# A scan with sums over a head's channels: gathers on column strips, one scan a step, products in pairs

## The chip, the cores and the metric

The kernel runs on one core of a Trainium2 chip. It is one long program of twelve stages, one after another, that keep the activations in SBUF from stage to stage. The metric is the device time of one execution in microseconds; the profile shows one execution instruction by instruction.

## The reference, cut to what matters

Of the twelve stages only the eighth, the linear attention with a decaying state, is touched. Per sequence (32 of them, 32 tokens each) and head (16 heads of 16 channels) it keeps a 16x16 state `S`:

```
k = sigmoid(x_norm @ key_w.T + key_b);  v, q = split(x_norm @ vq_w.T)
for each token s:                       # per sequence, per head
    S[d, e] = k[s, d] * S[d, e] + (1 - k[s, d]) * v[s, e]
    h[s, e] = sum over d of q[s, d] * S[d, e]
x = x + h @ out_w.T + out_b
```

Written with the difference to `v`, as the kernel does it, a step over one channel `e` is: spread `v[e]` (as a difference of neighbouring tokens) to the 16 partitions of its head, run a first-order scan along the tokens with the decay `k`, multiply with `q`, and sum over the 16 partitions of the head; `v` times the sum of `q` is added at the end.

## The kernel before, in words

Tokens lie along the free dimension, 512 to a half, and channels on the 128 partitions, so 8 heads are in a chunk. The 256 channels (two chunks) and 1024 tokens (two halves) make four quarters `i` (in the code `HALVES`), and each has 16 steps `e`, one for each channel of a head; `k` counts the 64 steps. A step goes through four engines:

- TensorE spreads (`spread_out`, L2344 and L2345): a 128x128 matrix of zeros and ones times the rounded differences and their rest, for two groups of 8 sequences of 33 columns each (`BIT` is 264). Each group goes into a PSUM bank of its own; three pairs of banks (`SLOTS`) rotate, so a spread waits for the scan three steps earlier.
- VectorE scans (L2459): `tensor_tensor_scan` over 264 columns, one instruction for each bank, from PSUM into one of four `state` buffers (`RING`). Column 0 of each sequence has a decay of zero, which starts the sequence afresh.
- GpSimd multiplies the state with the query (L2317), 512 columns into one of four `product` buffers.
- TensorE gathers (`gather_in`, L2356): an fp32 product of 128x128 weights `gather[:, e, :]`, with ones that send the 16 partitions of a head to output row `e` of that head, accumulated over the 16 steps of the quarter in a bank of `SUM`. It is issued three steps (`LAG`) behind the spread.

Between the steps lies the work of a quarter: `query_sums` (L2362) sums the query over a head on TensorE after step `QSUM`, `own_values` (L2431) multiplies that with `v` on VectorE, `results` (L2437) adds both out of PSUM into `hT` at step `EVICT` of the next quarter. In the third quarter, at the steps in `OUT`, TensorE multiplies the first four token tiles with the output weights (`project`, L2366) and VectorE adds them to `x` (L2441); the other four follow behind the loop. TensorE, VectorE and GpSimd each run their queue in the order written and wait on counting semaphores (`spread_done`, `state_ready`, `product_ready`, `gathered`, `own_ready`, `hT_ready`, `y_done`, `x_done`).

Ahead of the loop come the layer norm, the loads and twelve projections. SyncE loads the weights of the two next stages once the stage's own have come (`cw.sp`, `xw.sp`).

Of the kernel before, what the change touches and what calls it, by code (L numbers as in the profile page):

```python
# [6 lines left out]
ALU = mybir.AluOpType  # L7
# [8 lines left out]
P = 128  # L16
BATCH, SEQ, D = 32, 32, 256
# [4 lines left out]
HALF = 512  # L22
# [72 lines left out]
class Norm:  # L95


    HALVES = [range(0, TILES // 2), range(TILES // 2, TILES)]
# [199 lines left out]
class QuantWeights:  # L298


    PIECES, RING, FIRST, STEPS = 12, 3, 10, 8

# [1926 lines left out]
def stage_scan(core, cw, xw):  # L2229
    nc, d = core.nc, core.dram  # L2230
    HD = 16
    HALVES = CD * 2
    OWN = HALF // SEQ
    STEP = SEQ + 1
    BITS = 2
    BIT = OWN // BITS * STEP
    SLOTS = 3
    RING = 4
    LAG = 3
    EVICT, QSUM, OUT = 4, 6, (8, 10, 12, 14)  # L2240
    with ExitStack() as ctx:
        st = Stage(core, ctx, "scan")
        ln = Norm(st, shared=True)
# [1 line left out]
        wo = st.sb("wo", [P, CD, D])  # L2245
        bk = st.sb("bk", [P, CD])
        bo = st.sb("bo", [P, D])
        gather = st.sb("gather", [P, HD, P])
        same_head = st.sb("same_head", [P, P])
        decay = st.sb("decay", [P, HALVES, OWN, STEP])  # L2250
        vT = st.sb("vT", [P, HALVES, OWN, STEP])
        dv = st.sb("dv", [P, HALVES, OWN, STEP])
        spread_r = st.sb("spread_r", [P, HD, P], F32R)
        dv_hi, dv_lo = st.sb("dv_hi", [P, HALVES, OWN * STEP], F32R), st.sb("dv_lo", [P, HALVES, OWN * STEP], F32R)
        qT = st.sb("qT", [P, HALVES, HALF])
        own_v = st.sb("own_v", [P, 2, HALF])
        state = st.sb("state", [P, RING, OWN, STEP])
        product = st.sb("product", [P, RING, HALF])
        spread = product[:, :, :].rearrange("p r (e m) -> p (r e) m", m=P)
# [13 lines left out]
        hT_ready = st.sem("hT_ready")  # L2273
        y_done, x_done = st.sem("y_done"), st.sem("x_done")
        bank = [b[:, :] for b in core.bank]
        SPREAD, SUM = [bank[0:2], bank[2:4], bank[4:6]], bank[6:8]
        PROJ = [(kind, n, c) for n in range(2) for c in range(CD) for kind in ("v", "k", "q")]
        block = ctx.enter_context(nc.Block())

# [2 lines left out]

        def by_seq(a):
            return a.rearrange("p (b s) -> p b s", s=SEQ)

        @block.sync
        def _(sp):
# [12 lines left out]
        @block.gpsimd  # L2300
        def _(pool):
            for a in (decay, vT, dv):
                nc.gpsimd.memset(a[:, :, :, 0:1], 0.0).then_inc(first_zero, 1)
            ln.pool(pool)
            pool.wait_ge(loaded, 64)
            ln.all_ready(pool)
            for t in range(TILES):
                nc.gpsimd.tensor_tensor(core.x[:, t, :], core.x[:, t, :], bo[:, :], ALU.add).then_inc(bo_added, 1)
            pool.wait_ge(proj_taken, len(PROJ))
            pool.wait_ge(spread_ready, 1)  # L2310
            for i in range(HALVES):
                for e in range(HD):
                    k = i * HD + e
                    pool.wait_ge(state_ready, (k + 1) * BITS)
                    if k >= RING:
                        pool.wait_ge(gathered, k - RING + 1)
                    nc.gpsimd.tensor_tensor(by_seq(product[:, k % RING, :]), state[:, k % RING, :, 1:STEP], by_seq(qT[:, i, :]),  # L2317
                                            ALU.mult).then_inc(product_ready, 1)

        @block.tensor  # L2320
        def _(pe):
# [14 lines left out]
            def spread_out(k):  # L2336
                i, e = divmod(k, HD)
                if e == 0:
                    pe.wait_ge(lo_ready, i + 1)
                if k >= SLOTS:  # L2340
                    pe.wait_ge(state_ready, (k - SLOTS + 1) * BITS)
                for g in range(BITS):
                    now, to = slice(g * BIT, (g + 1) * BIT), SPREAD[k % SLOTS][g][:, 0:BIT]
                    nc.tensor.matmul(to, spread_r[:, e, :], dv_hi[:, i, now], start=True, stop=False)  # L2344
                    nc.tensor.matmul(to, spread_r[:, e, :], dv_lo[:, i, now], start=False, stop=True).then_inc(spread_done, 1)  # L2345

            def gather_in(k):
                i, e = divmod(k, HD)
                if e == 0 and i >= 1:
                    pe.wait_ge(own_ready, i)  # L2350
                if e == 0 and i >= 2:
                    pe.wait_ge(hT_ready, i - 1)
                if k == 3 * HD:
                    pe.wait_ge(x_done, len(OUT))
                pe.wait_ge(product_ready, k + 1)
                nc.tensor.matmul(SUM[i % 2], gather[:, e, :], product[:, k % RING, :], start=(e == 0),  # L2356
                                 stop=(e == HD - 1)).then_inc(gathered, 1)

            def query_sums(i):
                if i >= 1:  # L2360
# [11 lines left out]
            for k in range(HALVES * HD + LAG):  # L2372
                i, e = divmod(k, HD)
                if i < HALVES:
                    spread_out(k)
                if k >= LAG:
                    gather_in(k - LAG)
                if i < HALVES and e == QSUM:
                    query_sums(i)
                if i == 2 and e in OUT:  # L2380
                    t = OUT.index(e)
                    if t == 0:
                        pe.wait_ge(own_ready, 3)
                    else:
                        pe.wait_ge(x_done, t)
                    project(t, SUM[1])
# [32 lines left out]
        def _(dve):  # L2419
# [12 lines left out]

            def results(i):
                n, c = divmod(i, CD)
                dve.wait_ge(gathered, (i + 1) * HD)
# [9 lines left out]
            for k in range(HALVES * HD):  # L2445
                i, e = divmod(k, HD)
                if i >= 1 and e == EVICT:
                    results(i - 1)
                if e == QSUM + 1:
                    own_values(i)  # L2450
                if i == 2 and e - 1 in OUT:
                    add(OUT.index(e - 1), SUM[1])
# [1247 lines left out]
```

## Time and profile before

| | us |
|---|---|
| median of 3 runs | 1755.07 |
| lowest and highest run | 1753.1, 1763.58 |
| profiled execution, first to last instruction (span) | 1752.7 |
| busy over the span: TensorE, VectorE, ScalarE, GpSimd | 1579.5, 1061.8, 846.3, 773.6 |
| the 128 scans (L2459), first start to last end | 1193.21 to 1285.06 |

The profiled execution is not one of the three runs, and of its own time the span is what is given. Times in the rows count from the start of that span. PE is TensorE's matmul part, DVE is VectorE, ACT ScalarE, POOL GpSimd and SP SyncE; an fp32 matmul leaves two records. Matmuls are pipelined, so a record is longer than the distance to the next, and it is that distance, the pitch, which shows what a stream of them costs. PEclk is the granted TensorE clock as a share of 2.4 GHz.

### The profile page before, as it was taken

The page shows a single profiled execution, that of the slowest core. Times are in us where ns is not written, and L with a number is a line of the kernel's source. Part 1 is how long each engine was busy: PE and PEld are TensorE (multiplying, and loading weights), DVE is VectorE, ACT ScalarE, POOL GpSimd, SP SyncE. Part 2 cuts the span into 40 slices and gives each one's busy share as a digit, 9 for nine tenths or more (in the row PEclk, how much of TensorE's full clock was granted, in tenths as well). Part 3 has the DMA queues.
Part 4 walks back from the last instruction along what each step waited for, and adds up shares of the span by engine and source line. Part 5 has one row for each costly group of instructions (what it writes and reads, how often), then busy time and mean ns, then how long its engine had stood idle before and what let it go on. Part 6 is the DMA issues. An engine that isn't in the chain of part 4 may idle for free. (4 is left out here: it accounts for less than half of the span.)

```text
span 1752.7 us, 37478 instructions
## 1 busy us (share of the span) xinstructions
PE 1579.5 (90%) x13621; PEld 1342.1 (77%) x13621; DVE 1061.8 (61%) x2990; ACT 846.3 (48%) x2433; POOL 773.6 (44%) x926
## 2 busy tenths in 40 slices
PE   7999999888888999987999999989978978759998
PEld 6889898757557999966888888955648834539997
DVE  5887887456866888844877666738960232263332
ACT  5766666445336888842756666641003213114332
POOL 7655665243339999833211111226734311212332
PEclk9999999999998999999999999999989977879999
DMA  8555545120014343303533333335037263871221
GB/s 267 181 163 169 162 153 164 58 85 2 1 37 158 128 140 134 119 19 111 176 109 103 112 121 104 104 113 176 1 88 240 25 194 127 269 237 30 39 39 28
DMA packets 127223, 205.32 MB, mean 117 GB/s; under 512 B 21034, under 2 KB 92363, under 8 KB 126531
## 3 DMA queue, kind: packets, MB, share of 16 engines
q1 hardware_dynamic: 119016, 189.62, 33.3%
q0 software_dynamic: 6720, 8.79, 3.2%
q10 hardware_dynamic: 1306, 4.51, 0.8%
q8 instruction: 112, 1.84, 0.4%
q14 instruction: 69, 0.56, 0.1%
HBM read 162.54 MB, written 41.14 MB: 116 GB/s over the span
## 5 line engine op out<-in xcount | busy, mean ns | idle before, releaser
L883 DVE TENSOR_SCALAR xattn_oT<-banks,xattn_last 128x256 f32<-128x256 f32 x256 | 111.8, 478 | 90.5 <-PE banks L703 90.4
L789 ACT ACTIVATE xattn_probs<-banks,xattn_negmax 128x257 f32<-128x257 f32 x256 | 124.0, 484 | 61.4 <-DVE xattn_negmax L864 61.3
L794 ACT ACTIVATE xattn_probs<-xattn_probs,xattn_rsum 128x257 f32<-128x257 f32 x256 | 131.9, 515 | 1.4 <-DVE xattn_rsum L868 1.4
L1114 POOL TENSOR_SCALAR xattn_probs<-xattn_probs,xattn_rsum 128x257 f32<-128x257 f32 x128 | 119.9, 937 | 21.3 <-DVE xattn_rsum L1354 21.2
L864 DVE TENSOR_REDUCE xattn_negmax<-banks 128x1 f32<-128x257 f32 x256 | 106.6, 416 | 35.1 <-PE banks L676 33.5
L621 POOL COPY ctx_stat<-xattn_mv 128x2 f32<-128x2 f32 x32 | 6.0, 189 | 238.1 <-DVE xattn_mv L897 238.1
L873 DVE TENSOR_TENSOR xattn_probsT_lo<-banks,xattn_probsT_hi 128x256 fp32r<-128x256 f32 x256 | 105.1, 410 | 9.8 <-ACT xattn_probsT_hi L800 8.8
L800 ACT CAST xattn_probsT_hi<-banks 128x256 fp32r<-128x256 f32 x256 | 95.6, 374 | 31.7 <-PE banks L683 27.7
L683 PE MATMUL banks<-ident,xattn_probs 128*128 128x128 f32 x512 | 103.7, 285 | 3.2 <-ACT xattn_probs L794 2.7
L672 PE MATMUL banks<-xattn_ctxT,xattn_qk_hi 128*128 128x258 f32 x256 | 93.7, 366 | 0.5 <-DVE xattn_qk L860 0.5
L577 POOL TENSOR_SCALAR xattn_ctxT<-xattn_rawT 128x514 fp32r<-128x514 f32 x32 | 49.9, 1560 | 98.1 <-issue 92.9
L698 PE MATMUL banks<-xattn_probsT_hi,xattn_ctxN 128*128 128x256 f32 x256 | 84.9, 332 | 4.9 <-DVE xattn_oT L883 3.3
L2317 POOL TENSOR_TENSOR scan_product<-scan_state,scan_qT 128x512 f32<-128x512 f32 x64 | 75.7, 1183 | 27.8 <-DVE scan_state L2459 27.3
L3051 PE MATMUL banks<-moe_xinT,moe_w_now 128*128 128x128 f32 x736 | 86.8, 277 | 0.0
L210 ACT COPY xnT<-banks 128x512 f32<-128x512 f32 x40 | 21.3, 589 | 135.0 <-PE banks L190 135.0
L3051 PEld LDWEIGHTS banks<-moe_xinT,moe_w_now 128*128 128x128 f32 x736 | 85.1, 194 | 0.1
L654 PE MATMUL banks<-xattn_qT,xattn_wk 64*128 64x128 f32 x1024 | 73.3, 283 | 12.8 <-DVE xattn_qT L849 10.0
L3009 POOL DMA_INDIRECT out_dram<-moe_y_slots,moe_row_u x23 | 36.5, 1585 | 108.7 <-DVE moe_y_slots L3176 105.7
L3061 PE MATMUL banks<-moe_w,moe_hT 128*128 x368 | 83.1, 379 | 0.0
L2459 DVE TENSOR_TENSOR_SCAN scan_state<-banks,scan_decay 128x264 f32<-128x264 f32 x128 | 81.3, 689 | 1.3
L654 PEld LDWEIGHTS banks<-xattn_qT,xattn_wk 64*128 64x128 f32 x1024 | 62.2, 187 | 22.0 <-issue 12.6
L719 PE MATMUL banks<-xattn_oT,xattn_wv 128*64 128x128 f32 x1024 | 69.4, 278 | 10.2 <-issue 7.6
(517 smaller groups left out, 5228.7 us busy)
## 6 DMA issues: line engine op xcount, KB each, us to landing
xattn_ctxT<-ctx_partsT SPq DMA_DIRECT2D x64, 516.0 KB, 4.0
xattn_ctxN<-ctx_partsN SPq DMA_DIRECT2D x64, 384.0 KB, 4.1
ctx_partsT<-xattn_ctxT SPq DMA_DIRECT2D x32, 516.0 KB
moe_w<-in_L_ffn_W SPq DMA_DIRECT2D x16, 1024.0 KB, 13.8
ctx_partsN<-xattn_ctxN SPq DMA_DIRECT2D x32, 384.0 KB
moecap_w_early<-in_L_ffn_w SPq DMA_DIRECT2D x10, 1024.0 KB, 9.3
xattn_rawN<-in_ctx SPq DMA_DIRECT2D x32, 192.0 KB, 2.8
xattn_raw<-in_ctx SPq DMA_DIRECT2D x32, 192.0 KB, 4.4
```

The costliest lines, as they stand in the source:

```text
L654: mm = nc.tensor.matmul(bank[:, k * P:(k + 1) * P], wk_s[r, h // 2, g % 2 * P:(g % 2 + 1) * P], qT[r, h // 2, :], start=True, stop=True, t ...
L672: nc.tensor.matmul(out, unit(qk1[0]), part(0, 0), start=True, stop=False)
L683: mm = nc.tensor.transpose(TB[n % 2][:, c * P:(c + 1) * P], probs[:, n % RING, c * P:(c + 1) * P], core.ident[:, :])
L698: nc.tensor.matmul(OB[:, 0:2 * P], first_hi(c), hi[:, c], start=(c == 0), stop=False)
L789: nc.scalar.activation(probs[:, n % RING, :], SB[n % 2][:, 0:KV], ACT.Exp, bias=negmax[:, n % RING:n % RING + 1], accum_out=psum[:, n % RI ...
L794: nc.scalar.mul(probs[:, n % RING, :], probs[:, n % RING, :], rsum[:, n % RING:n % RING + 1]).then_inc(norm_ready, 1)
L800: nc.scalar.copy(probsT[0][:, n // 2 % PAIRS, :, n % 2, :], TB[n % 2][:, 0:2 * P].rearrange("p (c n) -> p c n", c=2)).then_inc(probsT_hi_r ...
L864: nc.vector.tensor_reduce(negmax[:, n % RING:n % RING + 1], SB[n % 2][:, 0:KV], AX.X, ALU.max, negate=True).then_inc(negmax_ready, 1)
L873: nc.vector.tensor_tensor(lo, TB[n % 2][:, 0:2 * P].rearrange("p (c n) -> p c n", c=2), hi, ALU.subtract).then_inc(probsT_ready, 1)
L883: nc.vector.tensor_scalar(oT[k][:, heads, b, :], by_head(OB[:, k * 2 * P:(k + 1) * 2 * P]), last[:, k, j * PER_TILE + b:j * PER_TILE + b + ...
L1114: nc.gpsimd.tensor_scalar(probs[:, n % RING, :], probs[:, n % RING, :], rsum[:, n % RING:n % RING + 1], None, ALU.mult).then_inc(norm_read ...
L3051: mm = nc.tensor.matmul(H[n % 2][k][:, f * P:(f + 1) * P], w1_now[:, c, at:at + P], xinT[:, n % 2, c, :], start=(c == 0), stop=(c == CD - 1))
```

## The change

- **Gathers.** One gather now takes four steps (`QUAD`): four products of 128x32 weights, each with its own step's `product`, into the 32 PSUM partitions of its own column strip (`tile_position`). Steps `e`, `e+1`, `e+2`, `e+3` go to strips 0 to 3, four quads accumulate over the quarter, and one signal stands for a quad. The output channels of a chunk come out in another order; the host permutes the value weights, the output weights, and the zero-one matrices to fit, and the `gather` table shrinks to a quarter.
- **Scan.** The two halves of a spread are written at the end of one bank and the start of the next, so that 528 columns are contiguous, and one scan reads them. One signal stands for a step in `spread_done` and `state_ready`.
- **Products.** GpSimd multiplies the states of two steps (`PAIR`) in one instruction of 1024 columns, the query repeated. Six states and eight products rotate.
- **Order.** `LAG` goes from 3 to 5 (plus the four of a quad), `results` from step 4 to 7, the query sums from 6 to 9, own values from 7 to 11, and the output products of the first four tiles from steps 8, 10, 12, 14 of the third quarter to 13, 15, 17, 19, over its end.

```diff
-    RING = 4
-    LAG = 3
-    EVICT, QSUM, OUT = 4, 6, (8, 10, 12, 14)
+    RING, PRODUCTS = 6, 8
+    PAIR, QUAD = 2, 4
+    LAG = 5
+    EVICT, QSUM, OWN_AT = 7, 9, 11
+    OUT = [2 * HD + o for o in (13, 15, 17, 19)]
...
-        gather = st.sb("gather", [P, HD, P])
+        gather = st.sb("gather", [P, HD, SEQ])
...
-        SPREAD, SUM = [bank[0:2], bank[2:4], bank[4:6]], bank[6:8]
+        SPREAD = [core.banks[:, k * BITS:(k + 1) * BITS, :].rearrange("p g n -> p (g n)")[:, HALF - BIT:HALF + BIT] for k in range(SLOTS)]
+        SUM = bank[6:8]
...
-            for i in range(HALVES):
-                for e in range(HD):
-                    k = i * HD + e
-                    pool.wait_ge(state_ready, (k + 1) * BITS)
-                    if k >= RING:
-                        pool.wait_ge(gathered, k - RING + 1)
-                    nc.gpsimd.tensor_tensor(by_seq(product[:, k % RING, :]), state[:, k % RING, :, 1:STEP], by_seq(qT[:, i, :]),
-                                            ALU.mult).then_inc(product_ready, 1)
+            for k in range(0, HALVES * HD, PAIR):
+                pool.wait_ge(state_ready, k + PAIR)
+                if k >= PRODUCTS:
+                    pool.wait_ge(gathered, (k - PRODUCTS) // QUAD + 1)
+                now, to = slice(k % RING, k % RING + PAIR), slice(k % PRODUCTS, k % PRODUCTS + PAIR)
+                query = by_seq(qT[:, k // HD, :]).unsqueeze(1).broadcast_to([P, PAIR, OWN, SEQ])
+                nc.gpsimd.tensor_tensor(product[:, to, :].rearrange("p r (b s) -> p r b s", s=SEQ), state[:, now, :, 1:STEP], query,
+                                        ALU.mult).then_inc(product_ready, 1)
...
-                    pe.wait_ge(state_ready, (k - SLOTS + 1) * BITS)
+                    pe.wait_ge(state_ready, k - SLOTS + 1)
...
-                pe.wait_ge(product_ready, k + 1)
-                nc.tensor.matmul(SUM[i % 2], gather[:, e, :], product[:, k % RING, :], start=(e == 0),
-                                 stop=(e == HD - 1)).then_inc(gathered, 1)
+                pe.wait_ge(product_ready, (k + QUAD) // PAIR)
+                for z in range(QUAD):
+                    mm = nc.tensor.matmul(SUM[i % 2][z * SEQ:(z + 1) * SEQ, :], gather[:, e + z, :], product[:, (k + z) % PRODUCTS, :],
+                                          start=(e == 0), stop=(e == HD - QUAD), tile_position=(0, z * SEQ))
+                mm.then_inc(gathered, 1)
...
-                if k >= LAG:
-                    gather_in(k - LAG)
+                if k >= LAG and (k - LAG) % QUAD == QUAD - 1:
+                    gather_in(k - LAG - QUAD + 1)
...
-                if i == 2 and e in OUT:
-                    t = OUT.index(e)
+                if k in OUT:
+                    t = OUT.index(k)
...
                 if k >= RING:
-                    dve.wait_ge(product_ready, k - RING + 1)
-                for g in range(BITS):
-                    dve.wait_ge(spread_done, k * BITS + g + 1)
-                    of = slice(g * OWN // BITS, (g + 1) * OWN // BITS)
-                    flat = lambda a: a.rearrange("p b s -> p (b s)")
-                    nc.vector.tensor_tensor_scan(flat(state[:, k % RING, of, :]), SPREAD[k % SLOTS][g][:, 0:BIT], flat(decay[:, i, of, :]), 0.0,
-                                                 ALU.add, ALU.mult).then_inc(state_ready, 1)
+                    dve.wait_ge(product_ready, (k - RING) // PAIR + 1)
+                dve.wait_ge(spread_done, k + 1)
+                nc.vector.tensor_tensor_scan(flat(state[:, k % RING, :, :]), SPREAD[k % SLOTS], flat(decay[:, i, :, :]), 0.0,
+                                             ALU.add, ALU.mult).then_inc(state_ready, 1)
```

## Rows read from the trace of the kernel before

**Rows 1.** Windows, middle of loop: stretch, busy of each engine, PEclk, DMA, GB/s

```profile
1220.00:1243.00 23.00, 23.00 (x101) 14.46 (x99) 22.08 (x36) 0.00 (x0) 19.51 (x17) 1.00 0.00 1
```

**Rows 2.** Groups by line, 1193 to 1287 us

```profile
L2459 DVE TENSOR_TENSOR_SCAN scan_state<-banks,scan_decay 128x264 f32<-128x264 f32 x128 | 81.3, 689 | 1.3
L2317 POOL TENSOR_TENSOR scan_product<-scan_state,scan_qT 128x512 f32<-128x512 f32 x64 | 75.7, 1183 | 27.8 <-DVE scan_state L2459 27.3
L2356 PE MATMUL banks<-scan_product,scan_gather 128*128 128x512 f32 x128 | 65.1, 593 | 0.6 <-POOL scan_product L2317 0.6
...
L2366 PE MATMUL banks<-scan_wo,scan_hT 128*128 128x256 f32 x16 | 4.1, 379 | 0.0
L2362 PE MATMUL banks<-scan_qT,scan_same_head 128*128 128x512 f32 x8 | 4.1, 592 | 0.0
...
L2431 DVE TENSOR_TENSOR scan_own_v<-banks,scan_vT 128x512 f32<-128x512 f32 x4 | 2.8, 691 | 1.6 <-PE banks L2362 1.6
...
L2441 DVE TENSOR_TENSOR x<-x,banks 128x256 f32<-128x256 f32 x4 | 1.7, 422 | 2.3 <-PE banks L2366 2.3
```

**Rows 3.** Timeline of PE, one step: start us, us, engine, line, idle before

```profile
1197.37 1.02 PE L2356 MATMUL banks<-scan_product,scan_gather 128*128 128x512 f32 x2
...
1198.35 0.28 PE L2345 MATMUL banks<-scan_dv_lo,scan_spread_r 128*128 128x264 f32 x1
...
1198.58 0.28 PE L2345 MATMUL banks<-scan_dv_lo,scan_spread_r 128*128 128x264 f32 x1
1198.71 1.02 PE L2356 MATMUL banks<-scan_product,scan_gather 128*128 128x512 f32 x2
```

**Rows 4.** Timeline, first spread product and first scans

```profile
1192.07 0.39 PE L2344 MATMUL banks<-scan_dv_hi,scan_spread_r 128*128 128x264 f32 x1 [0.68 <-ACT scan_qT L2410]
...
1193.21 8.47 DVE L2459 TENSOR_TENSOR_SCAN scan_state<-banks,scan_decay 128x264 f32<-128x264 f32 x14
```

**Rows 5.** Timeline, end of the loop

```profile
1282.41 2.65 DVE L2459 TENSOR_TENSOR_SCAN scan_state<-banks,scan_decay 128x264 f32<-128x264 f32 x4
...
1285.14 1.18 POOL L2317 TENSOR_TENSOR scan_product<-scan_state,scan_qT 128x512 f32<-128x512 f32 x1 [0.17 <-DVE scan_state L2459]
...
1287.53 0.69 DVE L2437 TENSOR_TENSOR scan_hT<-banks,scan_own_v 128x512 f32<-128x512 f32 x1 [2.47 <-PE banks L2356]
```

**Rows 6.** Timeline of PE, products on column strips in a later stage

```profile
1445.18 0.27 PE L3404 MATMUL banks<-ident,xattn_o_norm 128*128 128x128 f32 x1
1445.29 0.27 PE L3405 MATMUL banks<-ident,xattn_o_norm 128*64 128x128 f32 x1
1445.49 0.86 PE L3393 MATMUL banks<-xattn_N,xattn_probsT 128*32 128x194 f32 x16
...
1446.75 0.66 PE L3368 MATMUL banks<-xattn_T,xattn_qk 128*32 128x257 f32 x8
1447.21 0.64 PE L3369 MATMUL banks<-xattn_T,xattn_qk 66*32 66x257 f32 x8
1447.78 0.44 PE L3377 MATMUL banks<-ident,xattn_probs 128*128 128x128 f32 x2
```

**Rows 7.** Groups by line and shape, GpSimd, whole span

```profile
L1487 POOL TENSOR_TENSOR attn_probs<-attn_probs,attn_rsum 128x512 f32<-128x512 f32 x8 | 8.4, 1050 | 16.6 <-DVE attn_rsum L1683 16.6
...
L1784 POOL TENSOR_TENSOR attn_x_plus<-x,xn 128x2048 f32<-128x2048 f32 x1 | 4.5, 4525 | 0.6 <-DVE xn L155 0.6
```

**Rows 8.** Windows and timeline of PE in other stages

```profile
820.00:825.00 5.00, 3.06 (x20) 1.39 (x18) 3.36 (x18) 2.42 (x5) 2.69 (x4) 1.00 0.74 254
...
1305.00:1310.00 5.00, 0.42 (x8) 0.36 (x8) 4.19 (x21) 0.21 (x1) 0.00 (x0) 0.50 0.32 82
...
1465.00:1470.00 5.00, 5.00 (x27) 2.12 (x26) 0.00 (x0) 0.97 (x3) 0.33 (x2) 0.50 0.30 119
...
825.86 3.81 PE L636 MATMUL banks<-xnT,xattn_wq 128*128 128x128 f32 x32 [2.34 <-ACT xnT L210]
...
1463.60 0.47 PE L3404 MATMUL banks<-ident,xattn_o_norm 128*128 128x128 f32 x1 [1.45 <-ACT xattn_o_norm L3482]
```

More of the change, by code:

```diff
@@ L2257, in stage_scan @@
         state = st.sb("state", [P, RING, OWN, STEP])
-        product = st.sb("product", [P, RING, HALF])
-        spread = product[:, :, :].rearrange("p r (e m) -> p (r e) m", m=P)
+        product = st.sb("product", [P, PRODUCTS, HALF])
+        spread = product[:, 0:HD * P // HALF, :].rearrange("p r (e m) -> p (r e) m", m=P)
         hT = st.sb("hT", [P, CD, TOKENS])
@@ L2284, in by_seq, with flat @@
             return a.rearrange("p (b s) -> p b s", s=SEQ)
+        def flat(a):
+            return a.rearrange("p b s -> p (b s)")
         @block.sync
@@ L2340, in spread_out @@
                 if k >= SLOTS:
-                    pe.wait_ge(state_ready, (k - SLOTS + 1) * BITS)
+                    pe.wait_ge(state_ready, k - SLOTS + 1)
                 for g in range(BITS):
-                    now, to = slice(g * BIT, (g + 1) * BIT), SPREAD[k % SLOTS][g][:, 0:BIT]
+                    now = slice(g * BIT, (g + 1) * BIT)
+                    to = SPREAD[k % SLOTS][:, now]
                     nc.tensor.matmul(to, spread_r[:, e, :], dv_hi[:, i, now], start=True, stop=False)
-                    nc.tensor.matmul(to, spread_r[:, e, :], dv_lo[:, i, now], start=False, stop=True).then_inc(spread_done, 1)
+                    mm = nc.tensor.matmul(to, spread_r[:, e, :], dv_lo[:, i, now], start=False, stop=True)
+                mm.then_inc(spread_done, 1)
             def gather_in(k):
@@ L2434, in results @@
                 n, c = divmod(i, CD)
-                dve.wait_ge(gathered, (i + 1) * HD)
+                dve.wait_ge(gathered, (i + 1) * HD // QUAD)
                 dve.wait_ge(own_ready, i + 1)
@@ L2448, in _ @@
                     results(i - 1)
-                if e == QSUM + 1:
+                if e == OWN_AT:
                     own_values(i)
-                if i == 2 and e - 1 in OUT:
-                    add(OUT.index(e - 1), SUM[1])
+                if k - 1 in OUT:
+                    add(OUT.index(k - 1), SUM[1])
                 if k >= RING:
-                    dve.wait_ge(product_ready, k - RING + 1)
-                for g in range(BITS):
-                    dve.wait_ge(spread_done, k * BITS + g + 1)
-                    of = slice(g * OWN // BITS, (g + 1) * OWN // BITS)
-                    flat = lambda a: a.rearrange("p b s -> p (b s)")
-                    nc.vector.tensor_tensor_scan(flat(state[:, k % RING, of, :]), SPREAD[k % SLOTS][g][:, 0:BIT], flat(decay[:, i, of, :]), 0.0,
-                                                 ALU.add, ALU.mult).then_inc(state_ready, 1)
+                    dve.wait_ge(product_ready, (k - RING) // PAIR + 1)
+                dve.wait_ge(spread_done, k + 1)
+                nc.vector.tensor_tensor_scan(flat(state[:, k % RING, :, :]), SPREAD[k % SLOTS], flat(decay[:, i, :, :]), 0.0,
+                                             ALU.add, ALU.mult).then_inc(state_ready, 1)
             results(HALVES - 1)
@@ L3671 @@
     same_head = p[:, None] // HD == p[None, :] // HD
-    spread = same_head[:, None, :] & (p[:, None, None] % HD == np.arange(HD)[None, :, None])
-    data["spread"] = np.ascontiguousarray(spread, dtype=np.float32)
-    data["same_head"] = np.ascontiguousarray(same_head, dtype=np.float32)
-    data["gather"] = np.ascontiguousarray(spread.transpose(2, 1, 0), dtype=np.float32)
+    strip, place = p // SEQ, p % SEQ
+    at = place % (P // HD) * HD + place // (P // HD) * 4 + strip
+    chunks = np.concatenate([at, P + at])
+    vq = data["L2_attn_vq_w_T"]
+    data["L2_attn_vq_w_T"] = np.ascontiguousarray(np.concatenate([vq[:, 0:D][:, chunks], vq[:, D:]], axis=1))
+    data["L2_attn_out_w_T"] = np.ascontiguousarray(data["L2_attn_out_w_T"][chunks])
+    spread = same_head[:, None, :] & (p[:, None, None] % HD == np.arange(HD)[None, :, None])
+    data["spread"] = np.ascontiguousarray(spread[at], dtype=np.float32)
+    data["same_head"] = np.ascontiguousarray(same_head[:, at], dtype=np.float32)
+    own = np.stack([(at[e % 4 * SEQ:(e % 4 + 1) * SEQ] % HD == e)[None, :] & same_head[:, at[e % 4 * SEQ:(e % 4 + 1) * SEQ]]
+                    for e in range(HD)], axis=1)
+    data["gather"] = np.ascontiguousarray(own, dtype=np.float32)
     data["number"] = np.arange(512, dtype=np.float32)
```

## The prediction

> **What bounds the kernel now.** I read the busy shares by stretch first. In the middle of the scan loop the matmul engine is busy 23.00 of 23 us at full granted clock, VectorE 22.08, GpSimd 19.51, and the DMA engines are silent [rows 1]. All three engines are nearly full, so busy time alone doesn't name the bound. The groups by line do: GpSimd's product waits 27.3 us in total for VectorE's scan, while the scan has only 1.3 us of recorded idle time ahead of it [rows 2]. What the scan itself waits for shows in TensorE's timeline. There one step takes 1.34 us, from one gather (1197.37) to the next (1198.71), with no hole: four spread products that start 0.12 us apart (0.23 us for two, 1198.35 to 1198.58) are 0.48 us, and the fp32 gather runs as two records, 0.59 us long and together 1.02, so 0.43 us apart: 0.86 us [rows 2, 3]. So TensorE needs 64 x 1.34 = 85.8 us, plus four query sums of 0.86 us and four output products of about the same (4.1 us busy for each kind, overlaps with their neighbours counted in [rows 2]): 85.8 + 3.4 + 3.4 = 92.6 us. The loop lasts 91.9 us from the first scan at 1193.21 [rows 4] to the end of the last at 1282.41 + 2.65 = 1285.06 [rows 5]. TensorE fits.
>
> VectorE could go faster. Where spread sums lie ready, 14 scans follow each other in 8.47 us: (8.47 - 0.68)/13 = 0.60 us each, 1.20 us a step [rows 4]. Its other work in the loop is three evictions and four own-value products of 512 columns, 0.691 us, and four adds of 0.422 us, each followed 0.08 us before its recorded end as the scans are (0.68 - 0.60): 7 x 0.61 + 4 x 0.34 = 5.6 us [rows 2]. That is 76.8 + 5.6 = 82.4 us, 10.2 us below TensorE. GpSimd needs 64 x 1.18 = 75.5 us [rows 2].
>
> **The gathers on column strips.** A gather of one step fills all 128 output columns of the array's weights, though a step yields 8 useful rows. The change takes four steps as four products of 32 weight columns, each on its own strip. The records stay as many (128), so all depends on whether strips overlap. The nearest rows are the score products of a later stage: 128x32 weights, 257 columns, fp32. Eight records on four strips start at 1446.75 and the next eight at 1447.21, so 0.46 us for eight, and the sixteen are gone by 1447.78, 1.03 us [rows 6]. One after another at the gather's rate (0.43 us for 512 columns, 0.215 for 257) sixteen would take 3.44 us. Overlap is 3.3 to 3.7 of 4. Eight records of 512 columns then take 0.46 x 512/257 = 0.92 us. Going over from whole-array products to strips costs little there: a transpose at 1445.29 (0.11 us by the pitch of its neighbours) is followed by the first strip at 1445.49 [rows 6], 0.1 us late; I allow the same on the way back. A quad of steps thus costs 1.1 us on TensorE, where four gathers cost 3.44. TensorE's total falls to 64 x 0.48 + 16 x 1.1 + 6.8 = 55 us, far off the path.
>
> **One scan of 528 columns.** No row has one. VectorE's 256- and 512-column tensor operations with a PSUM operand last 0.422 and 0.691 us [rows 2], so 0.153 us of an instruction doesn't grow with its width. Two scans joined then last 2 x 0.68 - 0.153 = 1.21 us and follow each other every 1.13. Ends: 1.20 (nothing saved; the input also crosses from one PSUM bank into the next, which no row shows) and 1.05 (the 0.08 us of overlap saved once more). I take 1.13, since the two widths are the nearest rows. That a gain from joining can only be small is what the Trainium skill says too (DVE: opcode table, instruction layouts, handler registers and perf-mode slots, Datapath and trigger behaviour): the built-in scan runs at half throughput. By that rule, at the 0.96 GHz of its page Trainium Kernel Development and Optimization, NeuronCore Architecture, I estimate 264 columns at 0.55 us; the trace's pitch of 0.60 agrees and leaves 0.05 of it to save, for a joined pitch of 1.15 and a sum 1.3 us longer than the one below.
>
> VectorE's loop becomes 64 x 1.13 + 5.6 = 77.9 us against 91.9: **14.0 us less**. Its new waits cost nothing by this sum. One signal for both halves of a step delays only the first scan, and that one starts at 1193.21, over 1 us behind the first spread product at 1192.07 [rows 4], when a step's 0.48 us of them are long written. With three slots a spread may begin two scans (2.3 us) before it is read, and it takes 0.48 us, a quad 1.1 or a query sum 0.86 us between: the cover holds, and if a strip quad took over 1.7 us it would be gone. The eviction moves from step 4 to 7, its quad being issued at step 4 and done before step 6; the output products move past the half's end, one to every second step, and each finds its add done one step earlier. With those products spaced so, behind the waiting TensorE instruction stands one step's spread, not needed for over another step.
>
> **Products of two steps.** GpSimd's rows of 512 and 2048 columns, 1.183 and 4.525 us, give 2.18 ns a column and 0.07 us fixed [rows 2, 7]. A pair of 1024 columns then takes 2.30 us, 32 of them 73.5 us, under VectorE's 77.9. Ends: 2.10 (a 512-column product with a repeated operand takes 1.050 [rows 7]) and 2.37 (nothing saved). The pair's query is a repeated operand; that row speaks against a penalty. With six states, VectorE reuses a state four steps after its pair is complete, 4.5 us against 2.3: no wait. Eight products hold two quads, and a pair's place is freed by a quad issued about three steps earlier.
>
> What the pair costs is at the **end**. Now the last product begins 0.08 us behind the last scan (1285.14) and lasts 1.18; the last eviction starts at 1287.53, 2.47 us after the scans end [rows 5]. With pairs the last product is 2.30 us long, 1.1 more, and the last quad 0.1 to 0.2 us longer than one gather: **1.3 us more**. The output products behind it, and all later stages, keep their lengths; the loads of the next stages are done by the middle of the loop [rows 1], so nothing that was hidden comes out. The smaller gather table and the reordered weights touch loads and the host alone: nothing, as the loop starts behind projections on TensorE.
>
> **Sum.** 14.0 - 1.3 = 12.7 us off the profiled span of 1752.7 gives 1740.0. The median of the runs is 2.4 us above that span, which I take for what lies around it: 1742.4 us, 0.7% less.
>
> **Rivals.**
> 1. *VectorE or GpSimd takes the gain.* If the joined scan saves nothing, the loop is 64 x 1.20 + 5.6 = 82.4 us and the time 1747. If GpSimd is slow at pairs, its chain (2.3 us for the first two scans, 32 pairs, 1.3 for the last quad) passes VectorE's 77.9 + 3.8 from 2.44 us a pair; each further 0.1 us costs 3.2 us, and at 2.85 the time is that of before. For it: both engines are already at 85 to 96% busy [rows 1]. Against: GpSimd now waits for VectorE, and its two widths show a fixed part to save.
> 2. *The clock falls, and it ends slower.* TensorE would be occupied 55 of 78 us instead of all of it. Its granted clock stands at 1.00 (2.4 GHz) in a stretch with 3.06 of 5 us busy, but at 0.50 (1.2 GHz) in one with 0.42, and at 0.50 even in one with 5.00, after TensorE had waited 1.45 us [rows 8]. At half clock a step takes 0.96 + 2.1/4 = 1.49 us, all of TensorE's work 64 x 1.49 + 13.6 = 109 us; against the 95.5 us of now (1192.07 to the last eviction [rows 4, 5]) that is 13.5 us more: 1768. A step is then 109/64 = 1.70 us against 1.22 at full clock and 1.42 of now less the longer end, so it decides from two fifths of the loop at half clock on. For it: that stretch of rows 8. Against: TensorE's holes would be under 0.7 us, once a step, and behind a hole of 2.34 us at 825.86 the clock was still full [rows 8]. The Trainium skill's page TensorE: Matmul & The Clock Gate, Part 1, has throttled as the default state, which activity releases; rows 8 show both levels, so by that rule this rival stands.
> 3. *The strips run one after another* (the change then doesn't do what it says): a quad 3.6 us, a step 0.48 + 0.9 = 1.38, TensorE's work 64 x 1.38 + 6.8 = 95.1 us, 2.5 more than now, and behind the scans 1.3 us of product and 2.5 us of last quad on top: 1761. Rows 6 speak against it.
>
> **How the numbers follow.** The forecast's own band, with scan and pair between their ends, is 1738 to 1746: chance 0.73. Rival 1 (1746 to 1754): 0.15. Rival 2: 0.09, mostly in part (1750 to 1768). Rival 3: 0.03. The range 1738 to 1753 leaves out the upper parts of rivals 1 and 2, all of 3, and a little below. One per cent, about what a measurement of this kernel tells from no change, is 17.5 us: below 1737.5 needs the 1.05 scan together with 2.10 pairs or luck of the median (0.05); above 1772.6 nothing but the clock and more (0.03); within: 0.92.
>
> **What would show it.** After: 64 scans of about 1.21 us at a pitch of 1.13, GpSimd pairs of 2.30, gather records in bunches of eight within 1.1 us, TensorE waiting for the scan in most steps, clock 1.00, last eviction 3.8 us after the last scan. Wrong would be: scans with holes behind a GpSimd product, pairs above 2.44, gather records 0.43 us apart, or a granted clock of 0.50 in the loop.

## The result and the profile after

| | before | changed |
|---|---|---|
| median, us | 1761.74 (9 runs) | 1745.19 (9 runs) |
| lowest and highest, us | 1747.81, 1767.54 | 1742.32, 1759.40 |
| time of the profiled execution, us | not given (span 1752.7) | 1754.86 (span 1752.9) |

The ratio over all runs is 0.994 with a 95% interval of 0.9913 to 0.9967: 10.6 us of 1761.74 less, between 5.8 and 15.3. (The two medians alone are 16.6 us apart, the two means 11.1.) Against the forecast 0.7% it is 0.6%, and the median lies 2.8 us above the predicted 1742.4. The kernel before has a median of 1755.07 over its first three runs and of 1761.74 over all nine, so the ratio says more than the difference from one number.

The spans of the two profiled executions are equal all the same. In the one of after, the seven untouched stages ahead took 10.7 us more: the eighth begins at 1174.0 us instead of 1163.3, and over all profiled executions of this study it begins between 1162.6 and 1179.5. The total of one execution can't show a change of this size. From the first scan to the last instruction of the program the executions differ: 559.5 us before, 548.9 with the change and 548.5 for the same kernel again (e11), 10.6 and 11.0 less. But the stages behind vary too, between 455.1 and 460.0 us over the executions of the table. What shows the change best is the **stage by itself**, from the start of its first scan, and it repeats to 0.01 us (e11 against the changed kernel in the table). The first scan begins 29.9 to 30.0 us behind the stage's first VectorE instruction in all of them, so nothing of the change hides ahead of it. All times below are us from the first scan; "next stage" is the first VectorE instruction of the stage behind (its layer norm's statistics), and "end" is the stretch from the end of the last scan to the last eviction.

| kernel | last scan ends | last eviction | next stage | end | one execution |
|---|---|---|---|---|---|
| before | 91.85 | 94.32 | 99.57 | 2.47 | (span 1752.7) |
| changed | 79.08 | 83.38 | 91.37 | 4.30 | 1754.86 |
| e11_change_again | 79.08 | 83.38 | 91.36 | 4.30 | 1746.86 |
| e5_joined_alone | 91.99 | 94.46 | 99.71 | 2.47 | 1755.55 |
| e4_strips_alone | 83.24 | 85.67 | 92.50 | 2.44 | 1754.10 |
| e6_no_pairs | 80.77 | 84.08 | 91.17 | 3.31 | 1747.60 |
| e7_whole_gathers | 97.67 | 103.70 | 108.94 | 6.04 | 1767.42 |
| e1_filled_hole | 80.76 | 84.19 | 89.44 | 3.43 | 1748.42 |
| e2_single_end | 80.84 | 85.11 | 91.82 | 4.27 | 1745.93 |
| e3_both | 79.06 | 82.48 | 87.73 | 3.42 | 1742.46 |
| e8_busy_steps | 79.61 | 83.03 | 88.28 | 3.42 | 1755.30 |
| e9, e10 (e8 again) | 79.61 | 83.03 | 88.28 | 3.42 | 1746.08, 1745.54 |
| e12_single_busy | 79.58 | 82.02 | 87.26 | 2.44 | 1742.32 |

The loop is 12.77 us shorter, the end 1.83 longer, and from the last eviction to the next stage it takes 7.99 us instead of 5.25, 2.74 more: 12.77 - 1.83 - 2.74 = 8.20 us less for the stage. The groups by line of after, 1190 to 1290 us (against [rows 2]):

```profile
L2466 DVE TENSOR_TENSOR_SCAN scan_state<-banks,scan_decay 128x528 f32<-128x528 f32 x64 | 74.7, 1234 | 0.0
L2323 POOL TENSOR_TENSOR scan_product<-scan_state,scan_qT 128x1024 f32<-128x1024 f32 x32 | 70.0, 2186 | 21.6 <-DVE scan_state L2466 19.4
L2351 PE MATMUL banks<-scan_dv_hi,scan_spread_r 128*128 128x264 f32 x128 | 40.6, 340 | 13.0 <-DVE scan_state L2466 12.3 <-ACT scan_qT L2420 0.7
...
L2365 PE MATMUL banks<-scan_product,scan_gather 128*32 128x512 f32 x128 | 17.9, 633 | 3.9 <-POOL scan_product L2323 3.9
```

The scan has no idle time at all, and TensorE's spread (L2351) now waits 12.3 us for the scan. In the kernel before, the spread waited 0.8 us for it:

```profile
L2344 PE MATMUL banks<-scan_dv_hi,scan_spread_r 128*128 128x264 f32 x125 | 56.4, 471 | 0.8 <-DVE scan_state L2459 0.8
```

VectorE is the bound now. VectorE's own timeline says so directly, and gives the pitch:

```profile
1203.99 12.73 DVE L2466 TENSOR_TENSOR_SCAN scan_state<-banks,scan_decay 128x528 f32<-128x528 f32 x11
1216.64 0.67 DVE L2441 TENSOR_TENSOR scan_own_v<-banks,scan_vT 128x512 f32<-128x512 f32 x1
1217.22 13.87 DVE L2466 TENSOR_TENSOR_SCAN scan_state<-banks,scan_decay 128x528 f32<-128x528 f32 x12
...
1277.23 5.84 DVE L2466 TENSOR_TENSOR_SCAN scan_state<-banks,scan_decay 128x528 f32<-128x528 f32 x5
1287.37 0.69 DVE L2447 TENSOR_TENSOR scan_hT<-banks,scan_own_v 128x512 f32<-128x512 f32 x1 [4.30 <-PE banks L2365]
```

Eleven scans follow each other in 12.73 us: (12.73 - 1.234)/10 = 1.150 us. The next row starts 0.58 us behind 1216.64, without a hole, and no hole comes until the last eviction, which waited 4.30 us. TensorE's timeline around one gather of four steps (against [rows 3]):

```profile
1221.35 0.28 PE L2352 MATMUL banks<-scan_dv_lo,scan_spread_r 128*128 128x264 f32 x1
1221.56 1.07 PE L2365 MATMUL banks<-scan_product,scan_gather 128*32 128x512 f32 x8
1222.56 0.39 PE L2351 MATMUL banks<-scan_dv_hi,scan_spread_r 128*128 128x264 f32 x1
1222.79 0.28 PE L2352 MATMUL banks<-scan_dv_lo,scan_spread_r 128*128 128x264 f32 x1
```

The eight records of a quad take 1.07 us. From the last spread product ahead (1221.35) to the second behind (1222.79) it is 1.44 us, of which those two products are 0.24 by their pitch: a quad occupies TensorE for 1.20 us with the passages to strips and back, 0.30 a step instead of 0.86. Then the end of the stage (against [rows 5]), with the granted clock by stretch below it (columns as in [rows 1]):

```profile
1278.56 6.75 POOL L2323 TENSOR_TENSOR scan_product<-scan_state,scan_qT 128x1024 f32<-128x1024 f32 x3 [0.69 <-DVE scan_state L2466]
...
1280.79 1.07 PE L2365 MATMUL banks<-scan_product,scan_gather 128*32 128x512 f32 x8 [0.35 <-POOL scan_product L2323]
...
1285.36 1.94 PE L2365 MATMUL banks<-scan_product,scan_gather 128*32 128x512 f32 x8 [3.51 <-POOL scan_product L2323]
...
1288.11 6.47 PE L2376 MATMUL banks<-scan_wo,scan_hT 128*128 128x256 f32 x16 [0.81 <-DVE scan_hT L2447]
...
1295.36 1.41 DVE L142 BATCH_NORM_STATS2 moecap_ln_stats<-x 128x6 f32<-128x256 f32 x4 [0.32 <-PEq L2243]
```

```profile
1220.00:1230.00 10.00, 7.96 (x52) 4.85 (x50) 10.00 (x10) 0.00 (x0) 9.49 (x5) 1.00 0.01 2
...
1280.00:1284.00 4.00, 1.51 (x12) 0.39 (x10) 3.07 (x3) 0.00 (x0) 3.76 (x3) 0.93 0.00 0
1284.00:1288.00 4.00, 1.94 (x8) 0.20 (x8) 0.63 (x1) 0.00 (x0) 1.31 (x1) 0.50 0.00 0
1288.00:1296.00 8.00, 6.62 (x18) 5.04 (x18) 2.38 (x7) 0.00 (x0) 0.00 (x0) 0.64 0.00 0
```

The last scan ends at 1283.07, the last pair at 1285.31. Before the last quad TensorE has stood idle for 3.51 us, the clock is at 0.50 (1.2 GHz), and the same eight records take 1.94 us. It is still there when the output products begin: 6.47 us for sixteen. The kernel before had 3.72 for the same sixteen, at full clock:

```profile
1288.28 3.72 PE L2366 MATMUL banks<-scan_wo,scan_hT 128*128 128x256 f32 x16 [0.78 <-DVE scan_hT L2437]
```

```profile
1287.00:1293.00 6.00, 4.22 (x18) 2.96 (x16) 2.60 (x6) 0.00 (x0) 0.00 (x0) 1.00 0.00 0
```

### The profile page after: what moved, and what is told of

It reads as the page before. It is cut to its first block and busy times, and to the rows that moved or that the text cites. A ratio compares the mean times of both kernels' runs of the same rounds, so it can differ in the third digit from the quotient of the medians.

```text
span 1752.9 us, 37348 instructions
## 1 busy us (share of the span) xinstructions
PE 1559.6 (89%) x13621; PEld 1332.4 (76%) x13621; DVE 1054.2 (60%) x2926; ACT 846.2 (48%) x2433; POOL 767.9 (44%) x894
## 5 line engine op out<-in xcount | busy, mean ns | idle before, releaser
L654 PE MATMUL banks<-xattn_qT,xattn_wk 64*128 64x128 f32 x1024 | 73.3, 283 | 12.8 <-DVE xattn_qT L849 10.0
L2323 POOL TENSOR_TENSOR scan_product<-scan_state,scan_qT 128x1024 f32<-128x1024 f32 x32 | 70.0, 2186 | 21.6 <-DVE scan_state L2466 19.4
L636 PE MATMUL banks<-xnT,xattn_wq 128*128 128x128 f32 x512 | 71.2, 288 | 6.4 <-ACT xnT L210 4.2
```

What stands on the lines that cost most here:

```text
L654: mm = nc.tensor.matmul(bank[:, k * P:(k + 1) * P], wk_s[r, h // 2, g % 2 * P:(g % 2 + 1) * P], qT[r, h // 2, :], start=True, stop=True, t ...
```

## The experiments

My theory after this look: the loop is VectorE's, at 1.15 us a scan; the strips give the room, the joined scan takes it, and the pairs only add to the end; most of the missing 4.5 us is the hole of 3.5 us at the end, behind which the clock is at half. Rivals: the clock has nothing to do with the hole; the pairs are needed for the loop; the last pair is what makes the end long; one part alone would have done. `keep_busy(n, bank)` is a helper that the kernel has already: n bf16 products of 128x256 on TensorE whose result nobody reads.

**The end: hole and last pair.** Three kernels: e1 gives TensorE 24 idle products between the last quad but one and the last quad, e2 splits the last pair in two single products, and e3 does both.

```diff
 # e1, TensorE's loop, ahead of gather_in
+    if k == HALVES * HD + 1:
+        pe.wait_ge(state_ready, HALVES * HD - 2)
+        core.keep_busy(24, 2)
 # e2, GpSimd's loop
-    for k in range(0, HALVES * HD, PAIR):
+    for k in [*range(0, HALVES * HD - PAIR, PAIR), HALVES * HD - 2, HALVES * HD - 1]:
+        n = PAIR if k < HALVES * HD - PAIR else 1
```

> The changed kernel with 24 idle-work products of 128x256 bf16 on TensorE between the last quad but one and the last quad, in the 3.5 us hole. My theory: the clock fell to 0.50 at the end because TensorE had nothing to do for 3.5 us, and the half clock made the last quad 0.9 us and the output products 2.7 us longer. Then the clock stays at 1.00, the last quad takes 1.07 us instead of 1.94, the output products 3.7 instead of 6.5, and from the first scan to the next stage's first VectorE instruction it is 87.7 us instead of 91.4. Rival: the end is slow for another reason (strips at the end, the order of the banks): 91.4 as it was, or longer by the added work.

> The changed kernel with the last pair of products split into two single ones. My theory: the pair costs 1.0 us at the end (2.19 against 1.18 us), so from the first scan to the last eviction 82.4 us instead of 83.4; the hole on TensorE shrinks from 3.5 to 2.5 us, and if that is short enough for the clock the next stage begins 87 us behind the first scan instead of 91.4, else 90.4. Rival: the last quad waits for something else than the last product: 83.4 again.

> Both edits: the hole filled and the last pair split. My theory: 81.5 us from the first scan to the last eviction and 86.7 to the next stage (99.6 before the change, 91.4 with it), some 13 us less than the kernel before, a ratio of 0.9925. Rival (the end is slow for another reason): 90 to 91 us to the next stage and a ratio of 0.994 as the change.

The timeline of TensorE in e1, at its end:

```profile
1277.28 2.79 PE L50 MATMUL banks<-ident 128*128 128x256 bf16 x24
1280.85 1.07 PE L2365 MATMUL banks<-scan_product,scan_gather 128*32 128x512 f32 x8 [0.78 <-POOL scan_product L2323]
1282.73 3.72 PE L2376 MATMUL banks<-scan_wo,scan_hT 128*128 128x256 f32 x16 [0.81 <-DVE scan_hT L2450]
```

With the hole filled down to 0.78 us the quad takes 1.07 again and the output products 3.72. The end shrinks from 4.30 to 3.43, and the way to the next stage from 7.99 to 5.25, what it was before the change: 0.87 + 2.74 = 3.6 us. So the hole was the cause: of the executions on strips, in none of the six in which it is filled (e1, e3, e8, e9, e10, e12) is the end slow, and in all five in which it isn't (the changed kernel, e11, e2, e4, e6) the clock falls there. But e1's loop is 1.7 us longer than that of the changed kernel, though nothing in it was touched. VectorE's row behind its first hole, TensorE's timeline ahead of that, and the granted clock by stretch:

```profile
1218.74 6.99 DVE L2469 TENSOR_TENSOR_SCAN scan_state<-banks,scan_decay 128x528 f32<-128x528 f32 x6 [0.74 <-PE banks L2352]
```

```profile
1213.93 0.28 PE L2352 MATMUL banks<-scan_dv_lo,scan_spread_r 128*128 128x264 f32 x1
1214.70 0.48 PE L2351 MATMUL banks<-scan_dv_hi,scan_spread_r 128*128 128x264 f32 x1 [0.49 <-DVE scan_state L2469]
1214.98 0.42 PE L2352 MATMUL banks<-scan_dv_lo,scan_spread_r 128*128 128x264 f32 x1
...
1215.77 1.94 PE L2365 MATMUL banks<-scan_product,scan_gather 128*32 128x512 f32 x8
...
1220.74 1.06 PE L2365 MATMUL banks<-scan_product,scan_gather 128*32 128x512 f32 x8
```

```profile
1205.80:1211.80 6.00, 5.67 (x38) 3.13 (x30) 6.00 (x7) 0.00 (x0) 5.63 (x3) 1.00 0.72 173
1211.80:1217.80 6.00, 4.65 (x22) 2.30 (x21) 6.00 (x6) 0.00 (x0) 5.24 (x3) 0.75 0.04 7
...
1235.80:1241.80 6.00, 5.55 (x34) 2.81 (x33) 5.25 (x6) 0.00 (x0) 4.90 (x3) 0.76 0.01 3
```

The clock fell **inside the loop**, twice (windows of 0.75 and 0.76). The spreads from 1214.98 on last 0.42 instead of 0.28 us and the quad 1.94 instead of 1.06, the hole ahead of them is 0.49 us long, and VectorE waits 0.74 us for spreads each time. Each wait costs its 0.74 us and the 0.08 that scans otherwise overlap by, 1.64 for both, which is the 1.7. The two scans of cover hide the rest of the slow stretch.

e2 missed. TensorE's hole was to shrink to 2.5 us and stays at 3.48, and the end is 4.27, not 1 us shorter. The timeline of e2:

```profile
1268.81 6.73 POOL L2324 TENSOR_TENSOR scan_product<-scan_state,scan_qT 128x1024 f32<-128x1024 f32 x4 [0.70 <-DVE scan_state L2467]
...
1275.59 1.94 PE L2366 MATMUL banks<-scan_product,scan_gather 128*32 128x512 f32 x8 [3.48 <-POOL scan_product L2324]
```

GpSimd's last four instructions (two pairs, two singles) run without a gap from 1268.81 to 1275.54, while the scans end at 1273.32. When step 62 is scanned, 1.15 us before that, GpSimd is still at the pair before. It starts the first single at 1273.23, 0.1 us ahead of the last scan's end, so both singles follow, 2 x 1.18 us, as long as the pair was. The split saves nothing: e2's loop is 1.8 us longer, with two falls of its own, and e3's end is e1's within 0.01 us, 1 us longer than forecast. Without falls in its loop e3 reaches the next stage at 87.73, 11.8 us before the kernel before. Over 5 rounds it has a median of 1742.6 of 6 runs, against 1757.52 of 11: ratio 0.9916 (0.9893 to 0.994).

**No pairs.** e6 sets `PAIR, QUAD = 1, 4`; all else is as in the change.

> The changed kernel with single products on GpSimd all along. My theory: GpSimd needs 64 x 1.18 = 75.5 us, less than VectorE's 79.1, so the loop keeps 79.1 us, and the end is 1.0 us shorter: 82.4 us from the first scan to the last eviction. Rival: without pairs GpSimd becomes the bound or holds VectorE up in places: over 84 us, with holes in VectorE's scans that end at a product.

Its end is 3.31 us instead of 4.30: one product behind the last scan, not a pair, saves 1.0. The hole ahead of the last quad is 2.94 us, and the clock is at half behind it too:

```profile
1279.97 1.94 PE L2365 MATMUL banks<-scan_product,scan_gather 128*32 128x512 f32 x8 [2.94 <-POOL scan_product L2323]
1282.71 5.57 PE L2376 MATMUL banks<-scan_wo,scan_hT 128*128 128x256 f32 x16 [0.81 <-DVE scan_hT L2447]
```

The loop is 80.77, again with two waits for spreads (0.76 and 0.75 us) at falls of the clock; without these (0.84 and 0.83 with the lost overlap) it would be the 79.1 of the changed kernel. GpSimd's 64 single products of 1.186 us are 75.9, and that still fits beside VectorE's 79. The pairs gain nothing here; e12 against e8, below, shows it without falls.

**One part at a time.** e4 has the strips alone, in the order of the changed kernel (`PAIR` 1 and two 264-column scans a step, each with its signal), e5 the joined scan alone in the kernel before, and e7 takes the strips out of the change (its `gather` table is full-size again, so `bo` shares memory with `hT`):

```diff
 # e7: four whole-width products in place of four strips
-    mm = nc.tensor.matmul(SUM[i % 2][z * SEQ:(z + 1) * SEQ, :], gather[:, e + z, :], product[:, (k + z) % PRODUCTS, :],
-                          start=(e == 0), stop=(e == HD - QUAD), tile_position=(0, z * SEQ))
+    mm = nc.tensor.matmul(SUM[i % 2], gather[:, e + z, :], product[:, (k + z) % PRODUCTS, :],
+                          start=(e + z == 0), stop=(e + z == HD - 1))
```

> Of the three edits the column strips alone, in the order of the changed kernel: two scans of 264 columns a step, single products. My theory (TensorE was the bound before, VectorE is it now): the loop is 128 x 0.60 + 5.4 = 82.2 us and from the first scan to the last eviction 84.8 us (94.3 before, 83.4 with the whole change). Rival (VectorE was the bound before, and the joined scan made the gain): 94 us.

> The kernel before with the joined scan of 528 columns alone. My theory: TensorE still needs 92.6 us, so 94.3 us from the first scan to the last eviction as before, within 1, and VectorE has holes of some 0.2 us a step. Rival (VectorE was the bound): 3.2 us less, 91.1.

> The changed kernel with the strips undone: quads of four whole-array products, joined scans and pairs kept. My theory: TensorE is the bound again, a quad takes 3.4 us, longer than the three slots of spread sums cover, and the last quad is 2.5 us longer: 95 to 102 us from the first scan to the last eviction, slower than before. Rival (joined scans and pairs made the gain): 84 to 86.

The scan's row in the groups by line of each, e4 first, then e5, then e7:

```profile
L2467 DVE TENSOR_TENSOR_SCAN scan_state<-banks,scan_decay 128x264 f32<-128x264 f32 x128 | 78.0, 676 | 0.8 <-PE banks L2352 0.7
```

```profile
L2459 DVE TENSOR_TENSOR_SCAN scan_state<-banks,scan_decay 128x528 f32<-128x528 f32 x64 | 79.3, 1251 | 4.1
```

```profile
L2466 DVE TENSOR_TENSOR_SCAN scan_state<-banks,scan_decay 128x528 f32<-128x528 f32 x64 | 76.6, 1241 | 16.7 <-PE banks L2352 16.3
```

The joined scan alone changes nothing: 91.99 us for the loop, as TensorE sets the pace. The strips alone make the scans dense (0.8 us idle) and bring 8.6 of the 12.8 us; of the other 4.2, e4 lost 0.9 at two falls of the clock (waits of 0.43 and 0.29 us, and the overlap twice), and joining brings 3.3, which is 64 x 0.05, now that VectorE is the bound. e7 is worse than before: VectorE waits 16.3 us for spreads. The reason stands in TensorE's timeline:

```profile
1244.43 0.29 PE L2352 MATMUL banks<-scan_dv_lo,scan_spread_r 128*128 128x264 f32 x1
1244.55 3.60 PE L2365 MATMUL banks<-scan_product,scan_gather 128*128 128x512 f32 x8
1247.58 0.69 PE L2351 MATMUL banks<-scan_dv_hi,scan_spread_r 128*128 128x264 f32 x1
1248.11 0.28 PE L2352 MATMUL banks<-scan_dv_lo,scan_spread_r 128*128 128x264 f32 x1
```

Read as above, a quad that isn't on strips occupies TensorE for 1248.11 - 1244.43 - 0.24 = 3.44 us, longer than the two scans of 2.3 us that a spread is ahead, and after it TensorE has to wait for scans again (6.0 us in all). Four gathers in a bunch pay here only because the bunch is short. e7 has the order, the joined scan and the pairs of the change, so without the strips these together make no gain.

**Why the clock falls in the loop.** It had fallen in e1, e2, e4 and e6, but not in the changed kernel, e3, e5 or e7. e8 is e3 with two idle products in every step from the fourth on; e9 and e10 are the same again, e11 is the changed kernel again.

```diff
     pe.wait_ge(state_ready, k - SLOTS + 1)
+    core.keep_busy(2, k % SLOTS * BITS)
```

> The kernel with both edits at the end, and two idle-work products of 128x256 bf16 ahead of each step's spread on TensorE, into the slot that the spread overwrites. In four of six profiled executions the granted clock fell to about half twice in the loop, and VectorE waited 0.75 us for a spread each time. My theory: what TensorE does in a step is near the least that keeps its clock, and 0.2 us more in each step keeps it at 1.00: no hole in VectorE's row, 79.1 us for the loop, 87.7 to the next stage, in each of three executions. Rival: the falls come by chance from elsewhere: two of three executions have two holes and 80.8 us. The whole gains at most 1 us on the version without (1742.6).

> The same kernel once more, for a second profiled execution. My theory: no fall of the clock in the loop, 79.1 us. Rival: two falls and 80.8 us, with two chances in three.

> The same kernel a third time. My theory: no fall of the clock in the loop, 79.1 us. Rival: two falls and 80.8 us, with two chances in three.

> The changed kernel as it stands, for another profiled execution on this chip. My theory: two falls of the clock in the loop are likelier than none (80.8 us against 79.1), and the half clock at the end stands: a last quad of 1.94 us and output products of 5 to 6.5 us. Rival (the slow end was chance): 1.07 and 3.7 us.

The windows of e8, and VectorE's timeline at the only hole that it records:

```profile
1222.00:1232.00 10.00, 9.11 (x70) 5.73 (x72) 10.00 (x11) 0.00 (x0) 8.98 (x5) 1.00 0.16 27
...
1272.00:1282.00 10.00, 9.79 (x73) 6.47 (x72) 9.79 (x11) 0.00 (x0) 7.90 (x5) 1.00 0.01 2
```

```profile
1275.12 2.40 DVE L2471 TENSOR_TENSOR_SCAN scan_state<-banks,scan_decay 128x528 f32<-128x528 f32 x2 [0.21 <-PE banks L2354]
```

TensorE is busy 8.9 to 9.8 of 10 us (7.0 to 9.6 in the changed kernel), at full clock throughout; the price is 0.5 us around the output products, where TensorE is nearly full (9.79 of 10) and one spread comes 0.21 us late, others by less. With idle products no loop fell (e8, e9, e10, and e12 below); of the executions on strips without them four of seven did. If each had the chance 4/7, four in a row without would come in (3/7)^4 = 3% of cases, so the idle products likely help. These are not draws of one and the same chance, though: the kernels differ, and in both executions of the changed kernel the clock falls at the end 79.5 us behind the first scan, so they may count as one. e11 has no fall in its loop either, where I had expected two, and the same slow end as the first execution of the changed kernel (4.30, then 7.98 to the next stage).

e8 over 5 rounds: median 1741.75 of 6 runs against 1756.16 of 11, ratio 0.9909 (0.988 to 0.9937).

**The best of each.** e12 has no pairs, the busy steps, and 20 idle products ahead of the last quad.

> The best of the experiments put together: strips and joined scans as in the change, single products on GpSimd all along, the hole at the end filled with 20 idle-work products, and two of them ahead of each step's spread. My theory: the loop takes 79.1 to 79.6 us, the end 2.45 us instead of 4.30 (1.0 less for the last product, 0.87 less for the last quad), 87.3 us from the first scan to the next stage (99.6 before, 91.4 with the change), 1 us better than the pairs with both holes filled; a ratio of 0.9905. Rival: GpSimd's singles, 75.5 us of 79, hold VectorE up once TensorE is kept busy as well: over 81 us for the loop and no gain on 88.3.

TensorE and VectorE at its end:

```profile
1278.23 1.07 PE L2366 MATMUL banks<-scan_product,scan_gather 128*32 128x512 f32 x8 [0.52 <-POOL scan_product L2323]
1279.36 0.69 DVE L2451 TENSOR_TENSOR scan_hT<-banks,scan_own_v 128x512 f32<-128x512 f32 x1 [2.44 <-PE banks L2366]
...
1280.11 3.72 PE L2377 MATMUL banks<-scan_wo,scan_hT 128*128 128x256 f32 x16 [0.81 <-DVE scan_hT L2451]
```

In the stage it came out as forecast: end 2.44 us, next stage at 87.26, 4.1 us before the changed kernel's and 12.3 before the kernel before. Against e8 it differs in the pairs (and in 20 idle products for 24): the loop is as long within 0.03 us and the end 1.0 shorter. Over 5 rounds it has a median of 1745.27 of 12 runs, against 1756.87 of 17: ratio 0.9933 (0.991 to 0.9956), not the 0.9905 that I expected. The intervals of the changed kernel, e3, e8 and e12 overlap widely. That e12 is the best of them rests on the stage's times alone; the totals can't tell them apart.

## Why the prediction was right, and where it was not

- **What bounded the kernel.** Right. e5 shows it from the other side: a cheaper VectorE gains nothing as long as TensorE's gathers are whole.
- **Strips: 1.1 us a quad.** Right: 1.20 with the passages. Rival 3 is out. Its price was too low, though: e7 is 9.4 us slower in the stage, where rival 3 said 6, since the bunch is longer than the cover, and TensorE, once it is through, has to wait for scans again.
- **Joined scan: pitch 1.13.** The mis-sized term of the loop: 1.150, so 64 x 0.02 = 1.3 us. The part that doesn't grow with the width is less in a scan (2 x 0.676 - 1.234 = 0.12 us) than in the tensor operations I took it from (0.153). Against 2 x 0.60 it saves 0.05 us, not 0.07. The 1.15 that the half-throughput rule gave (the Trainium skill, DVE: opcode table, instruction layouts, handler registers and perf-mode slots, Datapath and trigger behaviour) is what the trace shows. The rest of VectorE's work was 0.3 us cheaper than the 5.6 (its 512-column operations are followed after 0.58 us, its adds after 0.31), and the loop fell by 12.8 us instead of 14.0. So much of rival 1 is true, and no more: VectorE takes 1.2 us of the gain, GpSimd nothing.
- **Pairs: 2.30 us.** 2.186, and with 1.184 for 512 columns that is 1.96 ns a column and 0.18 us fixed; the 2048-column row of another line [rows 7] was no guide to it. That VectorE hides the pairs was right, and that they cost about 1.1 us at the end too (1.0 by e6). What I didn't ask was whether they are needed: e6 and e12 do without.
- **The end: 1.3 us more.** It was 1.83: the pair 1.0 as forecast, and the last quad, for which I allowed 0.1 to 0.2, 0.87 for the clock.
- **"The output products behind it, and all later stages, keep their lengths."** This is the step that failed: 2.74 us more for the output products at half clock. It goes back to rival 2, where I put TensorE's holes at "under 0.7 us, once a step". In the loop that holds (two of 0.71, all others up to 0.49). At the end it doesn't: after the last quad but one TensorE waits for the scans and the pair behind them, 3.5 us, while before it had been busy with gathers until the end. I had costed the pair as length on the path, and not as a hole on the engine that stands behind it. The Trainium skill's page TensorE: Matmul & The Clock Gate, Part 1, has the throttled clock as the default that activity releases, and the end of this stage agrees: 0.50 at 1284 to 1288.
- **Rival 2** so came true in a small form, 3.6 us at the end in both executions of the changed kernel, and in e1, e2 and e6 1.7 or 1.8 us in the loop, in e4 0.9; far from the two fifths of the loop from which it would have decided.

The sum: 14.0 forecast less 1.3 (scan) plus 0.1 (VectorE's other work 0.3 cheaper, 0.2 back for the last scan's full length and roundings) is 12.8; the end and the output products take 1.83 + 2.74 where 1.3 was forecast; 8.2 remain of 12.7. The measured 10.6 us has both inside its interval, so the runs can't tell whether 8.2 or 12.7 is the change's worth; the stage's trace can. That the median came within 2.8 us of 1742.4 is luck in part.

**Open.** What sets off the falls inside the loop. In the four executions that have them the clock falls 4 us (e2, e4) or 17 us (e1, e6) behind the first scan, and again at 37 to 39 us. The changed kernel, e3 and e11 have the same holes there, within 0.1 us, and don't fall. Up to its first fall e1 runs the same instructions as the changed kernel, so the kernel's work alone doesn't decide it. That idle products prevent it rests on four executions and was not tried further.

## What to carry to other kernels

When work is taken off the engine that bounds a stage, draw its timeline once more with the new bound and look for the holes that it now has, at the end above all: here a hole of 3.5 us cost 3.6 us more by the slower clock behind it (over the five executions with such a hole, of 2.9 to 3.5 us, it was 1.6 to 3.6), and a few products without use took that away. A part that makes instructions fewer on an engine which is not the bound (the pairs) bought nothing here, and it cost its length where the stage drains. And if one execution's total varies by 15 us, judge a change of 10 us by the stage's own marks, and only then by many runs.

## What the runs showed of the hardware

- A scan of 528 columns that reads across two PSUM banks is as even as any: 1.23 us each, every 1.150 us, against 2 x 0.60 for two of 264.
- Four column strips of 128x32 fp32 weights and 512 columns: eight records in 1.07 us, against 3.60 for the same eight at whole width; with the passages to strips and back it is 1.20 against 3.44 us of TensorE, 2.9 times as fast.
- TensorE's granted clock stood at 0.50 behind holes of 2.94 (e6), 3.48 (e2) and 3.51 us. Behind one of 3.08 us (e4) the quad still ran at full clock, in 1.06 us, and the clock was at 0.50 for most of the output products. It fell as well within loops whose longest hole was 0.76 us; with two small products without use in each step it stayed at 1.00 in four executions of four.
- At half clock a strip quad takes 1.94 us instead of 1.07; sixteen output products, most of them at half clock, took 6.47 instead of 3.72.
